# Third and fourth edge pass of a four-layer graph network: each edge tile summed at its own fixed place of a PSUM bank, VectorE adding the places to the sums in SBUF, in place of a window summed at run-time offsets and written out by ScalarE

## What is computed

```python
# layer 3
msg = feat[src] * ci[src, None]
agg = segment_sum(msg, dst, num_segments=N) * cj[:, None]
h = where(in_deg[:, None] > 0, agg, feat);  h @ weight + bias
x = layernorm(x + h_out)
# layer 4
h = x @ W
msgs = h[src] * edge_weight[:, None]
agg = segment_sum(msgs, dst, num_segments=N)
y = layernorm(agg + bias) * gamma + beta
x = layernorm(x + y)
```

## Time and profile before

| | |
|---|---|
| Time, median of 3 runs | 4434.95 us (4428.1 to 4437.35) |
| Span of the profiled execution | 5246.3 us |
| POOL busy | 3200.4 us (61%) |
| PE / weight loads busy | 2714.9 us (52%) / 2473.5 us (47%) |
| DVE / ACT busy | 1982.1 us (38%) / 1353.8 us (26%) |
| Mean granted TensorE clock | 0.634 of full speed |
| First pass, first to last row fetch issued | 42.0 to 1410.5 us |
| Second pass | 1471.2 to 2717.4 us |
| Third pass | 2809.2 to 3997.5 us |
| Fourth pass | 4024.9 to 5213.1 us |

### The profile page before, as it was taken

How to read it: one execution, slowest core, us unless ns; L and a number is a source line. 1 busy time by engine, 2 the same in 40 slices (tenths; PEclk the granted TensorE clock), 3 DMA queues, 4 the chain that set the end, 5 groups by cost and what they waited for, 6 DMA issues and landing times.

```text
span 5246.3 us, 56090 instructions
## 1 busy us (share of the span) xinstructions
PE 2714.9 (52%) x15042; PEld 2473.5 (47%) x15042; DVE 1982.1 (38%) x4498; ACT 1353.8 (26%) x4318; POOL 3200.4 (61%) x3366
## 2 busy tenths in 40 slices
PE   6666676666756666566683543332334333333334
PEld 6666676666645555556552432222224222222234
DVE  3555545555655555555554111111113221122124
ACT  1121112222333333333343321211112121111113
POOL 4555555556356666666646666666665666666664
PEclk7676666767777777777785555555555555555555
DMA  7655555555433333333321111111112111111111
GB/s 193 156 142 140 148 137 139 149 143 144 125 94 85 81 84 83 82 83 83 83 60 42 35 35 35 35 35 35 35 35 46 35 36 34 35 35 34 35 35 44
DMA packets 337349, 409.90 MB, mean 78 GB/s; under 512 B 212224, under 2 KB 248691, under 8 KB 336957
## 3 DMA queue, kind: packets, MB, share of 16 engines
q0 software_dynamic: 133120, 245.58, 19.7%
q1 hardware_dynamic: 203933, 160.75, 11.7%
HBM read 386.26 MB, written 19.77 MB: 77 GB/s over the span
## 4 chain that ended last, share of the span: by engine, by line
another core or an unknown queue 32%; PE 19%; DVE 15%; POOL 14%; issue 14%; ACT 3%; DMA 1%; SPq 1%; ACTq 0%; DVEq 0%; POOLq 0%
POOL rows L563 14%; PE bank L655 10%; DVE same L1557 3%; DVE first_only L1256 2%; PE bank L669 2%; DVE first_only L1395 2%; DVE same L1256 2%; PE bank L668 1%; DVE prod L1325 1%; DVE score L1327 1%; DVE prod L1323 1%; PE bank L752 1%; DVE first_only L1264 1%; PE bank L759 1%
## 5 line engine op out<-in xcount | busy, mean ns | idle before, releaser
L655 PE MATMUL bank<-same,rows 128*96 128x128 f32 x4992 | 1059.8, 385 | 1468.8 <-issue 540.6
L655 PEld LDWEIGHTS bank<-same,rows 128*96 128x96 f32 x4992 | 917.5, 246 | 1593.7 <-issue 866.8
L563 POOL DMA_INDIRECT rows<-kv_table,src_idx x832 | 789.7, 949 | 610.0 <-DVE msg L1335 357.0
L563 POOL DMA_INDIRECT rows<-pair_table,src_idx x832 | 786.4, 945 | 520.5 <-issue 208.6
L563 POOL DMA_INDIRECT rows<-h_table,src_idx x832 | 788.7, 948 | 426.9 <-issue 235.0
L938 ACT COPY acc<-bank 96x511 f32 (+1 forms) x832 | 479.4, 576 | 2205.1 <-remote 1582.2
L563 POOL DMA_INDIRECT rows<-ci_table,src_idx x832 | 785.0, 943 | 412.6 <-issue 239.1
L1256 DVE TENSOR_TENSOR same<-bank,rank_col 128x512 f32<-128x512 f32 x624 | 420.6, 677 | 1000.7 <-remote 587.9
L1557 DVE TENSOR_SCALAR same<-iota_s,rank_col,src_hi 128x128 f32<-128x128 f32 x832 | 235.0, 359 | 906.7 <-remote 748.2
L655 PE MATMUL bank<-same,msg 128*105 128x128 f32 x1664 | 366.3, 391 | 384.5 <-ACT acc L940 362.7
L655 PEld LDWEIGHTS bank<-same,msg 128*105 128x105 f32 x1664 | 321.8, 268 | 398.2 <-DVE same L1256 200.9
(11 more groups left out here) (168 smaller groups left out, 2899.5 us busy)
## 6 DMA issues: line engine op xcount, KB each, us to landing
first_only<-in_attr_cols SPq DMA_DIRECT2D x104, 384.0 KB
first_only<-q_table SPq DMA_DIRECT2D x832, 48.0 KB
first_only<-rank_rows SPq DMA_DIRECT2D x104, 256.0 KB
first_only<-keep_rows SPq DMA_DIRECT2D x104, 192.0 KB
rows<-kv_table,src_idx POOLq DMA_INDIRECT x832
rows<-pair_table,src_idx POOLq DMA_INDIRECT x832
rows<-ci_table,src_idx POOLq DMA_INDIRECT x832
rows<-h_table,src_idx POOLq DMA_INDIRECT x832
```

The lines of the kernel that those rows point to most:

```text
L563: pool.indirect_dma_start(rows[:, k, j, 0:width], None, table, bass.IndirectOffsetOnAxis(ap=src_idx[:, t:t + 1], axis=0)).then_inc(rows_in ...
L655: mm = pe.matmul(out[0:nrow, here], left(j), right(j), start=(j == 0), stop=(j == TQ - 1), skip_group_check=True)
```

## The change

In the third and fourth pass PE no longer reads offsets. Tile j's matmul writes its own 128 columns of the bank (`j * P` to `(j + 1) * P`), each with `start` and `stop`, so the four tiles don't touch one another. ACT evicts nothing. Instead DVE, in a new `add_up`, reads four node numbers (the first target of each tile) into registers and makes four additions, tile by tile: 128 columns of the bank plus the 128 columns of `acc` at the tile's first node, written to the same columns of `acc`. Each of the four waits for the one before, since windows overlap. The last one counts `copied`. `add_up` of quad q-1 stands in DVE's stream behind the making of `same` of quad q, and ahead of the node work of the slot; the last quad's stands behind the pass.

Now that sums are added up, `acc` has to hold zeros first. `zero_tile` is cleared once by DVE at the start; ACT copies it over the 13 chunks of `acc` ahead of the third pass (behind its last table instruction and ahead of the pass's side work), and over chunk c again in the tail of the third pass behind the table instructions of chunk c (`clear`, `clear_last`). `add_up` waits for these through `cleared`.

```diff
             def spread(s, q, i, k):
-                at = offsets(q)
+                out = bank[2 + 2 * (k % 2)]
                 wait(pe, s.same_done, q + 1)
                 wait(pe, rows_in[k], s.rows + (i + 1) * 16 * TQ)
                 wait(pe, s.copied, q - 1)
-                window(bank[2 + 2 * (k % 2)], F, at, lambda j: rows[:, k, j, 0:F], lambda j: same[:, k % 2, j, :]).then_inc(s.agg_done.sem, 1)
+                for j in range(TQ):
+                    mm = pe.matmul(out[0:F, j * P:(j + 1) * P], rows[:, k, j, 0:F], same[:, k % 2, j, :], start=True, stop=True)
+                mm.then_inc(s.agg_done.sem, 1)
...
+            def clear(c):
+                act.copy(acc[0:F, c * CN:(c + 1) * CN].rearrange("p (o e) -> p o e", o=CT), zeros).then_inc(cleared, 1)
+            def clear_last():
+                act.copy(acc[0:F, NC * CN:ACC], zero_tile[0:F, 0:ACC - NC * CN]).then_inc(cleared, 1)
...
                         ins = act.mul(half[:, c % 2, m, :], xu[:, t, F:2 * F], r_all[:, t:t + 1])
                     ins.then_inc(d_table, 1)
+                    clear(c)
...
-                    spread(q, k, acc, F, bank[2 + 2 * (k % 2)], part_sum, s2.agg_done, s2.held, s2.copied)
...
+            act.wait_ge(zeros_done, 1)
+            for c in range(NC):
+                wait(act, c_turned, c + 1)
+                clear(c)
+            clear_last()
             act.wait_ge(ones_row, 1)
             rolled(act, third_pass, WITH_SIDE)
             for slot in (NQ, NQ + 1):
                 nodes4(slot)
+            wait(act, s2.copied, NQ)
+            clear_last()
...
-                    spread(q, k, acc, F, bank[2 + 2 * (k % 2)], part_sum, s3.agg_done, s3.held, s3.copied)
...
+                dve.memset(zero_tile[:], 0.0).then_inc(zeros_done, 1)
...
+            def add_up(s, q, k, base):
+                _, first = nc.values_load_multi_w_load_instructions(starts[0:1, bass.ds(q * TQ, TQ)], engines=[dve.engine], min_val=0,
+                                                                    max_val=NPQ - P, skip_runtime_bounds_check_because=NODES)
+                wait(dve, cleared, base + min(q + 1, NC + 1))
+                wait(dve, s.agg_done, q + 1)
+                for j in range(TQ):
+                    here = acc[0:F, bass.ds(first[j], P)]
+                    ins = dve.tensor_tensor(here, bank[2 + 2 * (k % 2)][0:F, j * P:(j + 1) * P], here, ALU.add)
+                    if j < TQ - 1:
+                        st.did(ins)
+                        st.settle()
+                ins.then_inc(s.copied.sem, 1)
+                wait(dve, s.copied, q + 1)
...
                     one_hot(same[:, k % 2], iota_over, rank_col, q, P).then_inc(s2.same_done.sem, 1)
+                    if q > 0:
+                        add_up(s2, q - 1, (k - 1) % GQ, 0)
                     if static(q):
                         for c in ripe(q, 2):
                             scale4(c)
...
             rolled(dve, third_pass, PLAIN)
+            add_up(s2, NQ - 1, GQ - 1, 0)
...
                     ins.then_inc(s3.same_done.sem, 1)
+                    if q > 0:
+                        add_up(s3, q - 1, (k - 1) % GQ, NC + 1)
...
             rolled(dve, fourth_pass, WITH_SIDE)
+            add_up(s3, NQ - 1, GQ - 1, NC + 1)
```

More of the change, by code:

```diff
@@ L140, in gnn_kernel @@
         iota_col = sb("iota_col", [P, 1])
-        ones = sb("ones", [P, P])
+        zero_tile = sb("zero_tile", [P, P])
         x_nodes = sb("x_nodes", [P, NT, F])
@@ L218, in gnn_kernel @@
         weight_col = src_hi
+        zeros = zero_tile[0:F].rearrange("p (o e) -> p o e", o=1).to_broadcast([F, CT, P])
         x_cols = acc_max[0:F1, 0:NPQ]
@@ L285, in gnn_kernel @@
         max_held, max_copied = sem("max_held"), sem("max_copied")
+        zeros_done, cleared = sem("zeros_done"), sem("cleared")
         edge_sems = [sem(n) for n in ("same_done", "agg_done", "held", "copied")]
```

## The result

| | median of the runs | lowest to highest | profiled execution, its span |
|---|---|---|---|
| before | 4436.15 us | 4428.1 to 4438.08 | 5246.3 (given), 4435.6 (taken later) |
| after | 4475.94 us | 4468.97 to 4480.73 | 4467.2 |

The ratio is 1.0084, 95% interval 1.0072 to 1.0096: the change costs 40 us by the medians, 32 to 43 by the interval. The profile of before in the earlier trace rows is like those from a chip on which this kernel takes some 5200 us, profiled or not (first experiment). Rows of before in the tails are read from a second profile of before, taken on a chip where it takes 4437.4 us. One execution of a4_third_only, at a granted clock of 1.00, took 6740 us where the other three took 4463 to 4470; it is left out of that kernel's ratio, and nothing here tells its cause.

The account below looks back on a forecast made before the run. GpSimd's fetch pace was taken to bound the runs (4403 us), except in the tails, where PE and ACT did. Third tail 26.5 plus fourth 14.7 made 41 us, so 4435 + 41 = 4476 us, range 4440 to 4520.

Parts of the forecast that it names:

- What bounds the runs: Whole kernel: GpSimd's fetches set the pace nearly all the way, 4403 us by summed paces against a median of 4434.95.
- Waits that the profiled execution has and the runs hardly have: The 811 us between profiled span and median: late releases in the profiled execution, nearly absent from the runs.
- The middle costs nothing: Middle of the passes: removed evictions and added additions stay hidden under GpSimd's 4.99 us a quad, with 5 us of cover.
- The third rival: Middle not covered, the 0.30 us between fetches being the profile's: +290 us, 4725, or some 4550 in part; chance 0.10.
- An addition: 0.283 us and a gap of 0.12, 1.6 together: DVE's `add_up`: four dependent additions over 128 columns with register addresses take 1.6 us a quad, bounds 1.25 and 2.1.
- Ring of the third tail 7.96 in place of 5.56: Third pass's tail: products, `nodes4`, `same`, additions and release in one chain, +2.4 us a slot, 26.5 us in all.
- the old ring: Tails of the kernel before: ACT's eviction 0.80 plus products, sum and release 4.76, 5.56 us a slot at 1.2 GHz.
- Ring of the fourth tail 6.93 in place of 5.56: Fourth pass's tail: DVE's side work, `nodes5`, `same` and additions in one chain, 1.37 us more a ring, 14.7 in all.
- Clearing costs nothing: ACT's zeroing of `acc` ahead of the third pass and in its tail: hidden, nothing; 8 us if not hidden.
- The sum: Whole kernel: 26.5 us for the third tail plus 14.7 for the fourth make 41 us, 4435 to 4476 us.
- Slack in the tail: Rival: slack in the tails hides the added work, 4435 within 9 us, needing an earlier ring of 7.5 us; chance 0.10.
- Late releases tied to the old form: Rival: late releases come from register-offset overlapping matmuls and vanish with fixed places, 32 us gained, 4418 us; chance 0.06.

Follow-up runs that it names:

- first experiment: The kernel before, unchanged, profiled once more on the chip of 5200 us; 5208.6 us, span 5206.8, median of 22 further runs 5192.41.
- a4_third_only: The changed kernel with the change in the third pass alone, the fourth in the old form; 4464.46 us, ratio to before 1.0072.
- b0_before: The kernel before, unchanged, profiled again on the chip of 5200 us; 5208.6 us, where further runs had a median of 5192.41.
- a3_old_tail_again: The changed kernel with old sums and evictions for the last twelve quads of both passes; 4426.83 us against 4427.03 before, ratio 1.0001.
- a5: The changed kernel with each addition doubled for quads 0 to 195 of both passes; 4479.35 us, ratio to before 1.0102.
- a6: The changed kernel with each addition doubled for the last twelve quads of both passes; 4512.44 us, ratio to before 1.0172.
- a2: The changed kernel with PE's sum ahead of the products and, in the third pass, `scale4` and `nodes4` one slot later on DVE; 4454.43 us, ratio to before 1.0045.
- a3_old_tail: The changed kernel with the old form for the last twelve quads of both passes, on the chip of 5200 us; 5187.18 us against 5192.41 before, ratio 0.9979.
- a1_sum_first: The changed kernel with PE's sum ahead of the products in the tails, on the chip of 5200 us; 5246.59 us, ratio to before 1.0104.
- a7: The changed kernel with `same` of the next quad made earlier on DVE in both tails; 4464.50 us against 4424.68 before, ratio 1.0090.

## Why the prediction was right, step by step

**What bounds the runs.** Right. 4403 us by the sum of paces against 4435.6 of the undisturbed profile, and the fetches 1.248 us apart in both kernels. "Waits that the profiled execution has and the runs hardly have": right in that the given runs lack them, wrong in that they would belong to the profiled execution: they belong to a chip or its state (on the chip of b0_before the other runs are as slow).

**The middle costs nothing.** Right: a3_old_tail_again, 1.0001. The cover is larger than I made it, since a5 hides 450 us more. That the fourth pass's middle would even give back some 5 us, by shorter fetches, I had not in the sum. The third rival, that the 0.30 us between fetches are the profile's, falls: spans with a profile and runs without one agree within 9 us.

**An addition: 0.283 us and a gap of 0.12, 1.6 together.** Measured 0.287, 0.42 apart where the next has a new register, and 1.54 for four, 1.60 with the release. The Trainium skill, "VectorE: DVE Perf Modes", section on the TRN2 errata, gives 291 ns by its formula, which the trace bears out within 4 ns; its DRAIN section, by which a semaphore after each costs nothing extra, gives 1.2 us for the four as an estimate, and the trace doesn't bear that out: 0.13 us stand between two of these. Where the next instruction needs no new register there is 0.03, as in the earlier trace rows and in a6.

**Ring of the third tail 7.96 in place of 5.56.** The links were all right (3.04, 2.61, 0.66, 1.6): measured 3.03, 2.61, 0.57, 1.60. `same` starts before L1295 has quite ended and is overlapped by the additions' start by 0.1 us, as its rows show. Together 7.81 in such a slot. The mis-sized term is the old ring: 5.48 to 5.55 at 1.2 GHz, right, but in some slots TensorE had 2.4 GHz, so that the mean was 5.13, near the 4.99 at which GpSimd delivers. The prediction has this case ("a rise would shorten both kernels' rings, the old one only down to GpSimd's 4.99"), but for both kernels at once; it came to the old one nearly alone. 2.4 us a ring became 2.6, 26.5 us in all became 28.9 by the rings, 29.9 by the tail.

**Ring of the fourth tail 6.93 in place of 5.56.** Measured 6.71 in most slots, 6.62 in the mean, in place of 5.14; 14.7 us became 16.3 by the rings, 15.7 by the tail. `nodes5` to the first addition is 2.08 where I added 2.24, for the same overlap. That `scale5` and `sum5` hide beside the products is right, with 0.27 us to spare. As DVE waits for 0.27 of the 6.71 us only, this tail is nearly bound by DVE's own work, which the prediction had for the fast clock alone.

**Clearing costs nothing.** Right within what a3 tells (it has all of it).

**The sum.** 41 us predicted, 40 measured, 45.7 by the two tails. Both rings of after were 0.2 to 0.3 us shorter than I made them and both of before 0.4, so the tails cost 5 us more than the sum has, and the middle of the fourth pass gave about as much back, for which the sum has no term. So the closeness to 4476 is in part luck; that the tails carry all of it is shown (a3, a4), and that DVE's chain is what they carry is shown by a6 (its length enters in full, in both tails) and, for the third tail, a2 (opened, 4 of 30 us are left). No run opens the chain of the fourth.

**The rivals.** Slack in the tail: fallen, the old ring was shorter than assumed, not longer. Late releases tied to the old form: fallen by a3_old_tail and a1_sum_first, where they stay.

**What stays open.** Why the fast clock came oftener in the old tails: over the rings the granted clock is 0.74 (third) and 0.68 (fourth) in the mean before, 0.60 and 0.55 after. In the stretches below (columns as above) before has 0.74 and 1.00 with PE busy 6.57 and 5.02 of 8 us, after 0.50 with 4.63. In the middle of the passes, where PE is busy 40 to 44%, both have 0.50. PE's busy time alone doesn't order the rows: another stretch of before has 0.52 with PE busy 6.55 of 8 us, another of after 0.71 with 4.83.

```profile
3300.00:3308.00 8.00, 6.57 (x30) 6.05 (x31) 4.16 (x18) 1.82 (x7) 6.17 (x7) 0.74 0.20 43
...
3325.00:3333.00 8.00, 5.02 (x31) 4.28 (x32) 6.68 (x31) 4.51 (x16) 6.17 (x7) 1.00 0.33 80
```

```profile
3300.00:3308.00 8.00, 4.63 (x16) 4.24 (x16) 4.66 (x20) 1.87 (x6) 6.17 (x7) 0.50 0.21 43
```

A tail in which PE waits more may keep the slow clock, which would make such a wait cost twice; the 0.81 of a2's third tail, whose rings are 2.6 us shorter than after's, fits that. No run holds the rest fixed and changes PE's work alone, so it isn't shown.

## What to carry to other kernels

Work moved from one engine to another costs nothing while a third engine sets the pace, and its full length where an in-order stream closes a ring through it; so look for the few places, heads and tails of passes, where the pace setter has run out, and walk the chain there instruction by instruction. Here some 450 us of DVE work in 392 quads cost nothing, and 28 us in 24 quads cost 46 in the tails. Where such a ring has room in it, as in the third tail, try the order of the stream first (a2 opens it with one slot of delay, and takes most of that tail's cost away). Where the engine works nearly all of the ring, as DVE does in the fourth tail, order gives little (1 us in a7), and less work on that engine is what is left; no run tried that. And when a profiled span is far from the runs' median, sum the paces and take another profile before building on its waits.

## What the runs showed of the hardware that I had not expected

The same kernel takes 4427 us on one chip and 5192 on another (medians of 13 and 22 runs), profiled or not. What is late on the slower are releases behind matmuls: evictions start over 2 us behind the quad's last matmul in 220 of 416 quads, up to 16.3 us, while instructions of the other engines take equally long on both (an eviction 577 ns there and 578 here, a one-hot matrix 677 and 678). Fixed places don't remove it (a1_sum_first). A register load on DVE takes 0.34 us, and an address from a new register puts 0.13 us between two dependent instructions instead of 0.03; the load shows only where nothing else runs beside it. And the clock that TensorE is granted goes up and down within one tail, from slot to slot: eight products of 2.93 us are followed by eight of 1.57.
